# One payload row for both experts of a token, filled one step later, in a routed mixture-of-experts block

## The reference: what is computed

```python
h = layer_norm(x, ln1_w, ln1_b)
attn = causal_softmax(h@Wq, h@Wk, scale C**-0.5) @ (h@Wv)   # 4 heads of 32
x = x + attn @ Wo + bo
nx = layer_norm(x, ln2_w, ln2_b)
noisy = nx @ Wr + br + noise * softplus(nx @ Wn + bn)        # 8 experts
idx = top_k(noisy, 2);  gate = softmax over the two chosen
non_skip = sigmoid(nx @ Wsk + bsk) <= 0.5
expert_out = sum over e of gate[e] * (relu(nx @ W1[e] + b1[e]) @ W2[e] + b2[e])
out = where(non_skip, x + expert_out, x)
```

## Time and profile before

| | |
|---|---|
| median of 3 runs | 804.82 us (804.17 to 807.13) |
| the profiled execution, its own time | 797.03 us |
| its span, first to last instruction | 795.3 us |
| mean granted PE clock | 0.875 |
| busy: PE, DVE, ACT, POOL | 72%, 72%, 61%, 52% |
| first and last scatter of the routing stage | 81.0 us, 468.7 us |

### The profile page before, as it was taken

One profiled execution on the slowest core, in us unless ns is written; L12 is line 12 of the kernel. 1 busy time (PEld: TensorE's weight loads), 2 busy tenths in 40 slices (PEclk: granted clock), 3 DMA queues, 4 the chain that ended last, 5 costly groups with the idle time before them and its releaser, 6 DMA issues.

```text
span 795.3 us, 31404 instructions
## 1 busy us (share of the span) xinstructions
PE 575.5 (72%) x11012; PEld 450.8 (57%) x11012; DVE 576.2 (72%) x2270; ACT 486.8 (61%) x979; POOL 415.8 (52%) x478
## 2 busy tenths in 40 slices
PE   0468998999998999998756209999999999720000
PEld 0246776776776776676645107777777777610000
DVE  3357878778788888878665626777777777718997
ACT  2357777677787788777654307888888888700000
POOL 3000767767766777777655740666666666630000
PEclk9978999999999999999986558999999999965555
DMA  9854332232332233235453247677666676319998
GB/s 96 239 161 136 90 102 87 75 100 69 93 97 72 89 100 100 65 101 115 106 161 98 89 169 286 230 232 235 234 233 235 231 236 230 124 35 326 331 334 262
DMA packets 147276, 127.32 MB, mean 160 GB/s; under 512 B 37538, under 2 KB 125699, under 8 KB 147232
## 3 DMA queue, kind: packets, MB, share of 16 engines
q1 hardware_dynamic: 110368, 89.99, 37.7%
q10 hardware_dynamic: 24576, 20.98, 8.6%
q0 software_dynamic: 12288, 15.77, 6.2%
HBM read 73.86 MB, written 62.78 MB: 172 GB/s over the span
## 4 chain that ended last, share of the span: by engine, by line
PE 38%; issue 19%; DVE 17%; POOL 12%; ACT 4%; DVEq 3%; DMA 2%; ACTq 2%; SPq 1%; POOLq 1%
POOL expert_rows L1136 11%; PE ps L505 6%; PE ps L548 4%; PE ps L626 3%; PE ps L627 3%; PE ps L628 3%; PE ps L638 3%; PE ps L639 3%; DVE z L1062 3%; PE ps L640 3%; PE ps L570 3%; DVE stats L831 3%; DVE z L1067 2%; PE ps L586 2%; DVE sc_m L874 1%
## 5 line engine op out<-in xcount | busy, mean ns | idle before, releaser
L1136 POOL DMA_INDIRECT expert_rows<-pay,rows_of x256 | 255.4, 998 | 184.8 <-DVE rows_of L930 101.9
L1148 POOL DMA_INDIRECT expert_results<-z,words x128 | 136.3, 1065 | 106.0 <-DVE z L1029 74.7
L676 ACT ACTIVATE z<-xres,shift,rstd 128x128 f32 (+1 forms) x256 | 105.1, 483 | 34.1 <-DVE shift L865 34.1
L1043 DVE TENSOR_TENSOR hlo<-h,hhi 128x512 fp32r<-128x512 f32 x128 | 89.8, 701 | 46.0 <-ACT hhi L789 44.3
L787 ACT ACTIVATE h<-ps,w1x 128x512 f32<-128x512 f32 x128 | 88.3, 690 | 35.2 <-PE ps L628 31.0
L789 ACT ACTIVATE hhi<-ps,w1x 128x512 fp32r<-128x512 f32 x128 | 87.3, 682 | 0.0
L548 PEld LDWEIGHTS ps<-pT,v_sb 32*32 32x32 f32 x4096 | 48.8, 104 | 62.4 <-issue 60.3
L548 PE MATMUL ps<-pT,v_sb 32*32 32x32 f32 x4096 | 59.2, 202 | 31.5 <-DVE sc_m L874 24.0
L505 PE MATMUL ps<-ident,z 128*128 128x128 f32 x256 | 45.3, 305 | 25.1 <-ACT z L676 19.3
L528 PE MATMUL ps<-kT,qT 32*32 32x32 f32 x4096 | 56.4, 201 | 4.6 <-issue 0.5
L638 PE MATMUL ps<-hhi,w2x 128*128 128x512 f32 x128 | 56.5, 442 | 4.2 <-issue 4.2
(11 more groups left out here) (147 smaller groups left out, 1321.1 us busy)
## 6 DMA issues: line engine op xcount, KB each, us to landing
w1x<-split_weights SPq DMA_DIRECT2D x33, 514.0 KB, 3.8
w2x<-split_weights SPq DMA_DIRECT2D x33, 512.5 KB
expert_results<-zeros SPq DMA_DIRECT2D x32, 512.0 KB
pay<-expert_rows SPq DMA_DIRECT2D x33, 264.0 KB, 3.6
xres<-in_r_x SPq DMA_DIRECT2D x32, 256.0 KB
split_weights<-w2x ACTq DMA_DIRECT2D x16, 512.0 KB
hhi<-expert_results SPq DMA_DIRECT2D x16, 512.0 KB, 5.5
hlo<-expert_results SPq DMA_DIRECT2D x16, 512.0 KB, 5.5
```

The costliest lines, as they stand in the source:

```text
L676: m = nc.scalar.activation(z[:, j:j + 1], tile(xres, n, j), ACT.Identity, bias=shift[:, which, j:j + 1], scale=rstd[:, which, j:j + 1])
L1043: ev.tensor_tensor(hlo[:, c], h32[:, c % 2], hhi[:, c].bitcast(F32), ALU.subtract).then_inc(s_h_lo, 1)
L1136: g.indirect_dma_start(rows, bass.IndirectOffsetOnAxis(ap=rows_of[:, odd, k * J + j:k * J + j + 1], axis=0), pay[:, odd, k, j, :], None, b ...
L1148: g.indirect_dma_start(results, bass.IndirectOffsetOnAxis(ap=words[:, slot, j:j + 1], axis=0), yrow[slot][:, j, :], None, bounds_check=K * ...
```

## The change

`pay` becomes four buffers of one row per token; two of them serve the routing stage. Both experts' scatters of a token read the same row. ACT copies z2 once (512 columns), in step t for tile t-3 instead of t-2, between kT and the z2 norms, and puts 2 * token into channel 128 from a table `words_all` made once at the start. DVE writes the two expert numbers into channels 129 and 130 of the row, in the place of `top_f`, and so waits for the buffer's scatters there instead of at `rows_of`. POOL's two small operations per tile and their semaphores go. In the expert stage the word is channel 128 plus 1 where channel 129, the first choice, isn't the block's expert (`exp_no`, one more instruction in the table of blocks). The pipeline, the count of scatters and their size stay.

```diff
-        top_f = sb("top_f", [P, K, J])
         hot = sb("hot", [P, K, J, E + 1])
         hot_any = sb("hot_any", [P, J, E + 1], BF16)
         rowno = sb("rowno", [P, J, E + 1])
         rowhot = sb("rowhot", [P, K, J, E + 1])
         rows_of = sb("rows_of", [P, 2, K * J], U32)
-        token = sb("token", [P, K, J])
-        pay = sb("pay", [P, 2, K, J, RW])
+        words_all = sb("words_all", [P, N // P])
+        pay = sb("pay", [P, 4, J, RW])
...
                     nc.scalar.activation(kT[:], ps[:, 6, :], ACT.Copy).then_inc(s_k_copied, 1)
+                n = t - 3
+                if live(n):
+                    wait(act, sent[odd], pair(n, odd, SENT))
+                    if isinstance(n, int) and n == 0:
+                        act.wait_ge(s_pay_zeroed, 1)
+                    nc.scalar.activation(pay[:, odd, :, 0:C], z2[:, odd], ACT.Copy)
+                    nc.scalar.activation(pay[:, odd, :, C], words_all[:, bass.ds(n * J, J)],
+                                         ACT.Copy).then_inc(s_pay_made, 1)
...
-                n = t - 2
-                if live(n):
-                    wait(act, sent[par], pair(n, par, SENT))
-                    nc.scalar.activation(pay[:, par, :, :, 0:C], z2[:, par].unsqueeze(1).to_broadcast([P, K, J, C]),
-                                         ACT.Copy).then_inc(s_pay_made, 1)
...
-                    ev.scalar_tensor_tensor(top_f[:], top_i[:, :, 0:K].rearrange("p j k -> p k j"), 1.0,
-                                            keep[:, bass.ds(n * J, J)].unsqueeze(1).to_broadcast([P, K, J]),
+                    wait(dve, sent[odd], pair(n, odd, SENT))
+                    if isinstance(n, int) and n == 0:
+                        dve.wait_ge(s_pay_zeroed, 1)
+                    experts_of = pay[:, odd, :, C + 1:C + 1 + K]
+                    ev.scalar_tensor_tensor(experts_of, top_i[:, :, 0:K], 1.0,
+                                            keep[:, bass.ds(n * J, J)].unsqueeze(2).to_broadcast([P, J, K]),
                                             ALU.add, ALU.mult).then_inc(s_route, 1)
                     dve.wait_ge(s_route, n * ROUTE + 8)
-                    ev.tensor_tensor(hot[:].rearrange("p k j e -> p (k j) e"),
-                                     top_f[:].rearrange("p k j -> p (k j)").unsqueeze(2).to_broadcast([P, K * J, E1]),
-                                     expert_no[:].unsqueeze(1).to_broadcast([P, K * J, E1]),
+                    ev.tensor_tensor(hot[:],
+                                     experts_of.rearrange("p j k -> p k j").unsqueeze(3).to_broadcast([P, K, J, E1]),
+                                     expert_no[:].unsqueeze(1).unsqueeze(1).to_broadcast([P, K, J, E1]),
                                      ALU.is_equal).then_inc(s_route, 1)
                     dve.wait_ge(s_route, n * ROUTE + 9)
...
-                    wait(dve, sent[odd], pair(n, odd, SENT))
...
+            ev.tensor_scalar(exp_no[:], exp_f[:], 1.0, None, ALU.add).then_inc(s_table, 1)
...
-                ev.tensor_copy(words[:, slot], xg[slot][:, :, C].bitcast(U32)).then_inc(s_words_kept, 1)
+                ev.scalar_tensor_tensor(words[:, slot], xg[slot][:, :, C + 1], exp_no[:, bass.ds(i, 1)],
+                                        xg[slot][:, :, C], ALU.not_equal, ALU.add).then_inc(s_words_kept, 1)
...
+            g.iota(words_all[:], [[K * P, N // P]], base=0, channel_multiplier=K,
+                   allow_small_or_imprecise_dtypes=True)
...
-            g.iota(token[:], [[1, K], [K * P, J]], base=0, channel_multiplier=K,
-                   allow_small_or_imprecise_dtypes=True).then_inc(s_token_next, 1)
...
-            g.iota(blank_u[:, :, C:C + 1], [[0, J]], base=FAR, channel_multiplier=0).then_inc(s_blank_word, 1)
+            g.memset(blank[:, :, C:C + 1], float(FAR)).then_inc(s_blank_word, 1)
...
-                    apart(pool, (sent[odd], pair(n, odd, SENT)),
-                                (s_token_next, n + 1))
-                    g.tensor_copy(pay_u[:, odd, :, :, C], token[:]).then_inc(s_word_made, 1)
-                    apart(pool, (s_word_made, n + 1))
-                    g.tensor_scalar(token[:], token[:], float(K * G), None, ALU.add).then_inc(s_token_next, 1)
                     apart(pool, (s_route, n * ROUTE + ROUTE),
                                 (s_pay_made, n + 1))
                     for k in range(K):
                         for j in range(J):
                             g.indirect_dma_start(rows, bass.IndirectOffsetOnAxis(
                                 ap=rows_of[:, odd, k * J + j:k * J + j + 1], axis=0),
-                                pay[:, odd, k, j, :], None, bounds_check=E * ER - 1,
+                                pay[:, odd, j, :], None, bounds_check=E * ER - 1,
                                 oob_is_err=False).then_inc(sent[odd], 16)
 
```

More of the change, by code:

```diff
@@ L166, in build @@
         exp_f = sb("exp_f", [P, MG + 1])
+        exp_no = sb("exp_no", [P, MG + 1])
         weights_at = sb("weights_at", [P, MG + 1], U32)
@@ L193, in build @@
         fin = [z1[:, 0], z1[:, 1], z2[:, 0], z2[:, 1]]
-        xg = [pay[:, i // 2, i % 2] for i in range(4)]
+        xg = [pay[:, i] for i in range(4)]
         yrow = [(z1, z2)[i // 2][:, i % 2] for i in range(4)]
@@ L259, in build @@
         s_rank_made = sem("rank_made")
-        s_token_next = sem("token_next")
         s_pay_made = sem("pay_made")
-        s_word_made = sem("word_made")
         s_sent0 = sem("sent0")
@@ L325, in build @@
         CONSTS = 16 * 11
-        TABLE = 16
-        pay_u = pay[:].bitcast(U32)
-        blank_u = blank[:].bitcast(U32)
+        TABLE = 17
         def pair(n, par, per):
@@ L992, in _ @@
                              ALU.is_lt).then_inc(s_table, 1)
-            dve.wait_ge(s_table, 13)
+            dve.wait_ge(s_table, 14)
             ev.tensor_reduce(fours_sum[:], fours_used[:], AX.X, ALU.add).then_inc(s_table, 1)
-            dve.wait_ge(s_table, 14)
+            dve.wait_ge(s_table, 15)
             ev.tensor_scalar(fours_sum[:], fours_sum[:], 1.0, 4.0, ALU.max, ALU.mult).then_inc(s_table, 1)
-            dve.wait_ge(s_table, 15)
+            dve.wait_ge(s_table, 16)
             ev.tensor_scalar(blocks_more[:], fours_sum[:], -4.0, None, ALU.add).then_inc(s_table, 1)
```

## The result

The changed kernel takes 808.91 us (median of 12 runs, 806.68 to 817.46), the kernel before 804.5 us in the runs beside it (12 runs, 798.47 to 811.04). The ratio is 1.0084, with a 95% interval of 1.005 to 1.0117: slower by 6.8 us, at least by 4.0 and at most by 9.4 (the two medians alone lie 4.4 us apart). The forecast was +9.4 us and 814.2 us.

What follows compares the result with a forecast made beforehand. The prediction took a closed loop through ACT, PE and DVE to bound the routing steps. +12.8 for ACT's two copies, -1.8 for weight-splitting steps and -1.65 for the tail gave +9.4 us, 814.2 us; range 809 to 819, wider 806 to 822.

Steps and rivals of the forecast that it cites:

- closed loop: Routing step: ACT from shift to oT, PE, DVE to the next shift add up exactly to the 11.53 us step.
- pair: 512- and 4-column ACT copies between kT and z2 norms: 0.62 us paid in full per full-clock step.
- dear small copy: Rival: the 4-column copy costs as much as a norm, 0.91 us a step together, 821 us; chance 0.10.
- sum over the stage: Routing stage: 21 full-clock steps at 0.62 us, less 0.6 slack, plus 0.35 for lower-clock steps: +12.8 us.
- split step: Last routing steps, which split expert weights: the payload copy leaves the chain ahead of the weight cut, gain 1.8 us.
- tail: POOL's last four scatter batches: without cast and token step, three gaps shrink by 0.55 us each, gain 1.65 us.
- What was to cost nothing: DVE's moved scatter wait, strided expert numbers, start iota, extra table instruction and word operation: hidden, counted at nothing.
- The clock: Rival: PE idles 0.6 us longer per step, so more steps run at 1.2 GHz; +20 us, 834; chance 0.09.
- The queue as bound: Rival: POOL's scatter queue sets the routing step, so removing its two operations gains 8 us, 797; chance 0.05.
- The hidden pair: Rival: the loop has 0.6 us of play, so only the tail gains, 801.4 us; chance 0.08.

Runs made afterwards that it cites:

- e8: Changed kernel with ACT's two payload copies in its idle time before the z1 norms, plain transfers replacing the scatters; ratio 0.7743 to the kernel before.
- e11: Changed kernel with ACT's two payload copies back at the end of its step, plain transfers replacing the scatters; 795.75 us, ratio 0.9908 to the kernel before.
- e9: Kernel before with 512- and 4-column ACTIVATEs added between kT and z2 norms, plain transfers replacing the scatters; 7.4 us above e6.
- e10: Kernel before with plain transfers replacing the scatters, e6 repeated on a chip like the first; 797.75 us, ratio 0.9942 to the kernel before.
- plain kernels: Versions of the kernel before or the changed kernel in which two ordinary transfers of the same bytes replace a tile's eight indirect scatters; e6 took 812.3 us.
- e6: Kernel before with plain transfers replacing the scatters, on a chip where the kernel before takes 1041.51 us; 812.3 us.
- e7: Changed kernel with plain transfers replacing the scatters, otherwise as it is; ratio 0.7806 to the kernel before, 0.5 us above e6.
- e2: Changed kernel, scatters kept, with ACT's two payload copies moved to its idle time before the z1 norms; 1037.22 us, ratio 1.0032 to the kernel before.
- e12: e7 with one more 512-column copy ahead of ACT's two payload copies; 833.87 us, ratio 1.0399 to the kernel before.

## Why the prediction was right, and where it was off

**The closed loop and the pair in it: right.** The stretch was to be 5.9 us and is 5.89 to 5.90 in 24 of the 25 steps (5.79 in the first); the price of the pair was to be 0.62 and is 0.61. PE takes z2 up at 0.05 to 0.06 us in the steps at full clock. The bound of 0.91 for a dear small copy is out: it lasts 198 ns on average, like its nearest row. The other way round, e8 and e11 show the stretch back at 5.28 with the pair elsewhere, e9 shows 5.90 with the pair alone. The estimate of the pair from the Trainium skill (ScalarE: Activation LUTs, What ACT_TABLE_LOAD costs) was 0.61 us: the trace agrees, with 619 and 198 ns for the two and 0.61 us on the path.

**The sum over the stage: 12.8 us was too much.** Steps at full clock were to be 12.1 to 12.2 us. They are 12.07 to 12.17 in 14 of 16, and 12.01 and 11.70 in the first and the last, 12.07 on average. The average of before's twenty was 11.56. So each pays 0.51 and not the 0.59 that I had in the sum with its slack taken off. Part of it is slack that I counted too low: in eight of the twenty PE takes z2 up 0.13 to 0.24 us late, 1.15 us in all beyond the usual 0.05, where I wrote off 0.6. Another part is a step of 12.18 us before (at 359.68), in which DVE takes 5.14 us from the residual to the next shift instead of 4.49. It comes to 20 x 0.51 + 5 x 0.13 + 0.6 for the first step, 11.5 us.

**The split step: right** in its direction and near in its size (2.0 us against 1.8; the clock differs there too, so the part of the copy isn't clean). e11 against e10 has that step shorter by 3.4 us with the copy halved, but with 2.4 us of stops of PE on issue in e10's.

**The tail: right.** 1.65 us were expected. The distances between the first scatters of the last four batches fell from 12.98, 11.74 and 11.48 us to 12.24, 11.17 and 10.84: 0.74, 0.57 and 0.64, together 1.95. The gap fell to the 0.30 us that stands between two scatters, which I had as the outer bound; I took it that the issue of the wait would stay. The three differences aren't the cast's alone: single scatters in these batches last longer, before and after (453.31 takes 1.94 us).

**What was to cost nothing** (DVE's moved wait, the strided expert numbers, the word from the expert number, one more table instruction): no cost found. e11 is not above e10, DVE has no wait for scatters in the changed kernel's profile, and the time from the last batch to the end is the same.

**Together**, with the clock's part as in before's trace: 11.5 - 2.0 - 1.95 = 7.5 us, beside the 6.8 (4.0 to 9.4) of the runs.

**The clock: mis-sized, and its cause misjudged.** I had it as a rival with PE idle 0.6 us longer in each step as its cause, and counted 3 steps either way. In the traces the number of steps at the lower clock goes from 5 to 9, worth 5.0 us. That is one trace of each. Over whole executions the granted clock of the changed kernel isn't lower: 0.865 to 0.881, median 0.872, in its 12, against 0.860 to 0.878, median 0.869, in the 23 of the kernel before beside e10, a chip with the same time. The plain kernels show the count falling with the same pair (9 of 22 steps to 3) and rising with one more copy (to 15). So more idle time of PE doesn't mean more such steps; the count changes with the length of the step, either way. That the medians differ by less than the traces fits with what before's profiled execution (797.0) lacks: the stop of PE, worth 4.3 us in the kernel before (15.26 in e6 against 10.97 in e10's same step), and some of the low-clock steps (4 of the 22, where its plain forms have 9), at 1.6 us each (13.20 less 11.56). One stop and two such steps would bring it to its median. For the clock's part the executions beside e10 speak too: the five of the kernel before with a granted clock of 0.875 or more take 797.7 to 799.7 us, those with 0.863 or less 802.9 us and more. How the 7.5 us divide isn't shown: no other execution of before has a trace here.

**The place of the forecast.** I added the 7.8 us by which before's trace lay under its median to a sum made in steps of that trace. Where the median run has more steps at the lower clock, as I argue, the change's 0.5 us a step doesn't hold for those (five of them paid 0.13 each). With two more of them, and with the stop, in whose step the pair costs nothing, 7.5 becomes 6.1 us, between the 4.4 of the medians and the 6.8 of the ratio. This too is argued and not shown. 814.2 was too high by 5.3 us. Its own range (809 to 819) just misses 808.91; the wider one, drawn to take in the dear copy, holds it. The mechanism was right, the terms mis-sized were the sum over the steps (12.8 for 11.5) and the step's price carried to the median; that the wider range still held the time is partly luck, since its lower end wasn't drawn for that.

**The rivals.** The queue as bound is refuted by e6 and e8, and by POOL's waits for rows in the changed kernel. The hidden pair is refuted by the step of 12.07 us with PE waiting for z2, and by e7 against e8. What stays open: what makes the clock fall in one step and not in the next; what stops PE on issue once near the start; and the time of the full kernel with the pair in the idle place where its loop is closed. In the plain form that place gains about 6.3 us over the changed kernel's (e7, e8); with the scatters it ran only where PE's supply sets the step, and there it gained nothing (e2).

## What to carry to other kernels

Before moving work to an engine's "free" place, follow one step around the engines and see whether its durations add up exactly to the step: what lies inside such a loop costs its full price, what lies in the wait of the same engine costs nothing. The same two instructions cost about 6.3 us more at the one place than at the other (e7, e8). The share of waits or the chain of one queue doesn't show this: POOL's chain looked like the bound and wasn't.

Price a change at every level of the clock that its steps run in, and don't take the difference of two single traces for its price: here the traces said 15.5 us and the medians 4.4, and 3.7 of the 15.5 came with a stop of PE that the kernel before has too, in other executions. And where an experiment's kernel before doesn't take its usual time, look at what has become the bound before reading any ratio.

## What the runs showed of the hardware

- On three chips the issue of PE's 32x32 matmuls stood still again and again while POOL's indirect scatters ran (gaps of 0.5 to 2.1 us, over soon after the eight scatters are), and a step took 20.3 us, the kernel before 1032 to 1042. On one of them the scatters were taken out and the step fell to 11.5. On the chips of the first and the last runs the same program takes 803 to 805, and leaving the scatters out gains 5.4 us (on the one where it was tried) instead of 229. Why the chips differ was not found.
- Steps of one and the same loop run at two clocks in a pattern that depends on the length of the step: of 22 steps 9 to 12 with a step of 11.5 us, 3 to 5 with 12.1, 15 with 12.6 (plain kernels); with the scatters 4 with 11.5 and 8 with 12.1, one trace each. A step with a fall costs 0.9 to 1.6 us more. So a longer loop can cost less (e7, 5.1 us in 22 steps where 0.59 a step makes 13) or more than its instructions (e12, +36 us where 22 to 25 steps of 1.1 us make 24 to 28).
- PE can stand 2.3 to 2.9 us on issue in the middle of a run of 32x32 matmuls, with 0.50 of its clock granted behind it (80 to 86 us after the change). Seven of nine traces have this once or twice at 79 to 107 us, with indirect scatters and without. It costs 3.7 us (15.30 against 11.59) to 4.3 (15.26 against 10.97).
- An ACTIVATE of 4 columns takes 0.20 us, and one of 512 columns 0.62, of which 0.10 and 0.10 lie under the next.
